# Gate columns beside W1 with routing one iteration later, POOL's products with D in the pair's own iteration, and expert rows filled up at the front

## What is computed

```python
mod = (silu(c) @ wmod).reshape(1, 6, 1, 512);  sa, ca, ga, sb, cb, gb = mod[:, 0], ..., mod[:, 5]
# the magnitudes of ga and gb are held at 0.25 or more
h = layernorm(x) * (1 + ca) + sa
x = x + ga * (tanh(h @ B.T) @ C.T + D * h)
h = layernorm(x) * (1 + cb) + sb
scores = sigmoid(h @ gate_w.T)                       # 2048 x 8
_, idx = top_k(scores + router_bias, 2)
w = take_along_axis(scores, idx); w = w / sum(w)
y_e = (silu(h @ W1[e]) * (h @ W3[e])) @ W2[e]        # inner width 352, for the 2 experts of a token
shared = (silu(h @ sw1.T) * (h @ sw3.T)) @ sw2.T     # inner width 704
x = x + gb * (sum_e w_e * y_e + shared)
```

## Time and profile before

| | us |
|---|---|
| median of 3 runs | 610.11 |
| the runs | 609.97, 610.11, 612.59 |
| the profiled execution | 610.75 |
| its span, first to last instruction | 609.1 |
| mean granted clock of TensorE | 0.981 of full |
| PE busy | 565.2 (93%), 3304 instructions |
| DVE busy | 321.6 (53%) |
| POOL busy | 242.4 (40%) |
| ACT busy | 178.1 (29%) |

### The profile page before, as it was taken

One profiled execution on the slowest core, in us unless ns is written; L12 is line 12 of the kernel. 1 busy time (PEld: TensorE's weight loads), 2 busy tenths in 40 slices (PEclk: granted clock), 3 DMA queues, 4 the chain that ended last, 5 costly groups with the idle time before them and its releaser, 6 DMA issues.

```text
span 609.1 us, 11649 instructions
## 1 busy us (share of the span) xinstructions
PE 565.2 (93%) x3304; PEld 508.9 (84%) x3305; DVE 321.6 (53%) x642; ACT 178.1 (29%) x332; POOL 242.4 (40%) x201
## 2 busy tenths in 40 slices
PE   4986899999999885999989999989999999999995
PEld 2655888988988774899979999979999998999994
DVE  3599788878876874432222222222222226666766
ACT  1344243344344131232222322223222322121220
POOL 1698674674683361340073500266160003322231
PEclk9998899999999988899999999999999999999999
DMA  8985193222222226952268632567662234554443
GB/s 312 369 278 207 52 346 123 87 103 97 75 104 104 102 91 223 345 209 96 85 216 317 230 121 80 161 216 268 239 224 71 69 101 143 163 170 151 141 140 116
DMA packets 37576, 102.72 MB, mean 169 GB/s; under 512 B 4272, under 2 KB 4272, under 8 KB 36656
## 3 DMA queue, kind: packets, MB, share of 16 engines
q1 hardware_dynamic: 27968, 53.65, 25.4%
q0 software_dynamic: 9152, 47.98, 22.1%
q10 hardware_dynamic: 432, 0.79, 0.3%
HBM read 71.73 MB, written 30.67 MB: 168 GB/s over the span
## 4 chain that ended last, share of the span: by engine, by line
PE 67%; issue 12%; DVE 9%; POOL 5%; DMA 4%; ACT 2%; SPq 1%; DVEq 0%; POOLq 0%; ACTq 0%
PE bank L808 11%; PE bank L810 11%; PE bank L809 11%; PE bank L822 6%; PE bank L824 6%; PE bank L823 6%; PE bank L794 4%; PE bank L829 3%; PE bank L899 2%; POOL wlo L474 2%; PE bank L764 2%; PE bank L763 2%; PE bank L765 2%; DMA whi<-w_all 2%; DVE sel L1087 1%
## 5 line engine op out<-in xcount | busy, mean ns | idle before, releaser
L808 PE MATMUL bank<-whi,thi 128*128 x416 | 140.2, 337 | 4.6 <-POOL wlo L474 4.6
L810 PE MATMUL bank<-whi,tlo 128*128 x416 | 135.2, 325 | 0.0
L809 PE MATMUL bank<-wlo,thi 128*128 x416 | 135.1, 325 | 0.0
L822 PE MATMUL bank<-whi,gth 128*128 (+1 forms) x204 | 81.6, 400 | 3.2 <-DVE gtl L1064 1.6
L808 PEld LDWEIGHTS bank<-whi,thi 128*128 128x128 f32 x416 | 79.1, 190 | 5.8 <-issue 5.8
L474 POOL TENSOR_TENSOR wlo<-raw,whi 128x1408 f32 (+3 forms) x21 | 69.0, 3308 | 35.4 <-DMA whi<-w_all 35.3
L1434 DVE TENSOR_TENSOR gbuf<-s,bank 128x352 f32<-128x352 f32 x52 | 27.0, 519 | 103.7 <-ACT s L742 103.4
L1438 DVE TENSOR_TENSOR gtl<-bank,gth 128x384 fp32r<-128x384 f32 x52 | 29.0, 558 | 97.8 <-ACT gth L746 97.8
L824 PE MATMUL bank<-whi,gtl 128*128 (+1 forms) x204 | 80.5, 395 | 0.0
L823 PE MATMUL bank<-wlo,gth 128*128 (+1 forms) x204 | 80.5, 395 | 0.0
L809 PEld LDWEIGHTS bank<-wlo,thi 128*128 128x128 f32 x416 | 79.3, 191 | 0.0
(11 more groups left out here) (180 smaller groups left out, 1046.0 us busy)
## 6 DMA issues: line engine op xcount, KB each, us to landing
raw<-w_all POOLq DMA_DIRECT2D x7, 2176.0 KB, 9.2
whi<-w_all POOLq DMA_DIRECT2D x14, 704.0 KB, 10.0
h<-xs_rows SPq DMA_DIRECT2D x36, 256.0 KB, 2.8
ys_rows<-tmpa SPq DMA_DIRECT2D x36, 256.0 KB, 2.1
x_all<-wmod SPq DMA_DIRECT2D x6, 1024.0 KB, 8.4
whi<-w_all POOLq DMA_DIRECT2D x7, 768.0 KB, 13.1
hs_rows<-h SPq DMA_DIRECT2D x8, 512.0 KB, 2.8
h<-hs_rows SPq DMA_DIRECT2D x16, 256.0 KB, 2.7
```

Of the source, the lines that this page charges most:

```text
L808: pe.matmul(dst, xh[:, j, a], wh, start=(m == 0), stop=False)
L809: pe.matmul(dst, xh[:, j, a], wl, start=False, stop=False)
L810: mm = pe.matmul(dst, xl[:, j, a], wh, start=False, stop=(m == KD - 1))
L822: pe.matmul(dst, gth[:, a], wh, start=(m == 0), stop=False)
```

## The change

Three parts.

**The gate.** The 8 gate columns are laid beside the 352 columns of W1 in slot A (`UPA = UP + E`), so that `up` of half 0 has 360 columns and the first 8 of its result are the gate's logits. ACT copies them out (`lg`) behind each silu, and makes the sigmoid at the end of the iteration. The 16 gate matmuls and the two `xtf` copies are left in one iteration only, that of the last pair (`it` = 10). Routing of pair p runs one iteration later: all of `route` and the scatter work on `it-4`, steps 7 to 11 stand together at the end of DVE's iteration, and PE's `ranks` stand behind the last `turn_g`. In iteration 10 the pairs 6 and 7 are both routed and both scattered.

**The term with D** of pair `it` is made in iteration `it`, behind `rs1`; before, it was made at the head of iteration `it+1`.

**The pads.** Each expert's rows now begin 128 rows further, and the zeros stand in the first 128 rows: one DMA of 2 MB near the start writes them for all experts. The first tile of an expert begins in the zeros (`lead`), which costs a few more small operations in `table_rows` and one in `routed`. The eight pads at the end of phase A are gone.

The core of the diff:

```diff
-PAD_ACT = 3
+UPA = UP + E
+SH = KD * E
...
+            sp.dma_start(xs[0:E * R, :].rearrange("(e r) d -> r e d", r=R)[0:P],
+                         zrow[:, :].unsqueeze(1).to_broadcast([P, E, D])).then_inc(s_pad, 16)
             sp.wait_ge(s_mod, 6)
...
-                if live(3, lo, hi):
-                    p = it - 3
+                if routes(lo, hi):
+                    p = it - 4
                     left = value(sp, p * 64)
                     sp.wait_ge(s_nat, p * 16 + 16)
...
+                if is_last(lo):
+                    sp.wait_ge(s_nat, NP * 16)
+                    sp.wait_ge(s_xd, NP)
+                    sp.dma_start(hrow[1], hs[(NP - 1) * 2 * P:NP * 2 * P, :].rearrange("(b p) d -> p b d", p=P)
...
-            pad(sp, 0, E - PAD_ACT, s_pad)
-            sp.wait_ge(s_pad, 16 * (E - PAD_ACT + 2))
-            sp.wait_ge(s_pad_act, 16 * PAD_ACT)
+            sp.wait_ge(s_pad, 48)
             sp.wait_ge(s_scat, 64 * NP)
...
             def body(it, lo, hi):
-                if lo > 2:
-                    with_d(it, lo, hi)
...
+                if lo > 2 and live(0, lo, hi):
+                    times_d(it)
+                    with_d(it)
...
+                if is_last(lo):
+                    scatter(it - 4, 0)
+                    scatter(it - 3, 1)
+                if routes(lo, hi) and not is_last(lo):
+                    scatter(it - 4, 0)
...
-                act.activation(s1[:, :], bank[2][:, 0:F], ACT.Silu).then_inc(q["A", "silu"], 1)
+                act.activation(s1[:, :], bank[2][:, E:E + F], ACT.Silu).then_inc(q["A", "silu"], 1)
+                if not is_last(lo):
+                    act.activation(lg[:, bass.ds(p * 2 + j, 1), :].rearrange("p a e -> p (a e)"), bank[2][:, 0:E],
+                                   ACT.Copy).then_inc(s_lg, 1)
...
                 if live(3, lo, hi):
                     hidden(it - 3, 1, lo)
+                    if not is_last(lo):
+                        p = it - 3
+                        act.wait_ge(s_lg, p * 2 + 2)
+                        act.activation(sc[:, bass.ds(p * 2, 2), :], lg[:, bass.ds(p * 2, 2), :],
+                                       ACT.Sigmoid).then_inc(s_sc, 1)
...
+                        if sec == "A":
+                            w, n = m * UPA + h * (E + F), F + (1 - h) * E
...
                 if live(3, lo, hi):
                     product_a(it - 3, 1, lo)
-                between(7, 8, 9)
                 if live(3, lo, hi):
                     finish_a(it - 3, 0, lo)
-                between(10)
                 if live(3, lo, hi):
                     low_a(it - 3, 1, lo)
-                between(11)
+                between(*range(KM + 1, KR))
```

More of the change, by code:

```diff
@@ L285, in live, with routes @@
             return lo - lag >= 0 and hi - lag < NP
-        def pad(eng, first, end, done):
-            eng.wait_ge(s_cnt, 1)
-            for e in range(first, end):
-                n = eng.value_load(ti[0:1, TB_N + e:TB_N + e + 1], min_val=0, max_val=T)
-                eng.dma_start(xs[bass.ds(n + e * R, P), :], zrow[:, :]).then_inc(done, 16)
+        def routes(lo, hi):
+            return lo - 4 >= 0 and hi - 4 < NP - 1
         def steps(eng, iters, step):
@@ L931, in body @@
                 if live(3, lo, hi):
+                    if not is_last(lo):
+                        pe.wait_ge(s_lg, (it - 3) * 2 + 1)
                     up("A", it - 3, 1, 0)
[L933 to L934 removed]
                 if live(3, lo, hi):
@@ L943, in body @@
                     turn_g(bank[5]).then_inc(q["A", "gt"], 1)
+                if routes(lo, hi) and not is_last(lo):
+                    ranks(it - 4, bank[7])
             pe.wait_ge(s_silb, KD)
```

204 lines of the change are left out of this document (108 added, 96 removed).

## The result

The changed kernel takes **612.63 us** (median of 20 runs, 610.63 to 614.24), the kernel before 610.50 (median of 20, 609.27 to 613.11). The ratio is **1.0029**, interval 1.0019 to 1.0038: slower by 0.3 %, within the 0.5 % that the prediction calls no change. Forecast were 607.0 and a range of 602.8 to 610.9; the time lies above it, and on the other side of the kernel before. The profiled execution of the changed kernel took 610.72 (span 609.0), 1.9 under its median. A second profile of the same kernel (experiment e13, span 612.2, 613.88 us) lies 1.3 over it, so I read both.

What follows compares the result with a forecast made beforehand. PE was taken to bound most inner iterations of phase A. Terms 0 + 1.5 + 3.4 - 2.2 + 0.35 = 3.05, say 3.1 us gained, brought the median from 610.11 to 607.0, range 602.8 to 610.9.

Steps and rivals of the forecast that it cites:

- Iterations 5 to 8: Phase A: `ra` held by POOL until 2.1, `up` starting at 4.6; gain 0.86 us each, 3.4 in all.
- `ra`, `pos` and `idx` take 0.5: DVE, iterations 5 to 8: these routing steps take 0.5 us after POOL's hold ends at 2.1, so `tlo` starts at 2.6.
- 5.3, where almost nothing is left: Iterations 5 to 8: late end of the forecast start of `up`, 5.3 us, with almost no gain left; 4.6 was taken.
- The first rival: Iterations 5 to 8: the hold misses the path, giving 1.5 us each, 2.6 more in all, 604.4; chance 0.18.
- Iteration 4: Phase A: `up` starts at 3.95 instead of 5.41, with wider half and hidden `ranks` counted; gain 1.5 us.
- The rival of a dearer switch of tables: ACT, iterations 4 to 8: table switch costs a wait behind `gth` too; 0.25 us gain each, 610.7; chance 0.03.
- Iteration 3: PE waits for the weights' third low half; a POOL product coming between offsets DVE's missing routing steps; gain 0.
- the third rival: DVE is held in more places, at iteration 3 by two products and at its head: 608.3 to 611.5; chance 0.12.
- Iteration 9: Phase A: POOL's work 0.8 us later, PE's wait 3.5, then slow clock taken as 1.5; loss 2.2 us.
- the rule of the port: Iteration 9: by it `sel` passes between two POOL instructions, gaining about 1.6 us; not used, the measured row was followed.
- The end: Iteration 10 to phase S: pads go, eight scatters land at 24.7 instead of pads at 25.07; gain 0.35 us.
- 4.4 would be there: End of phase A: far end of the gain, 4.4 us, if the scatters of pair 6 cost nothing.

Runs made afterwards that it cites:

- e13: Changed kernel again, nothing changed, on another chip: 613.57 us, ratio 1.0038.
- e8: Changed kernel with the routing's `ra`, `pos` and `idx` moved behind `xal` of the next iteration: 605.62 us, ratio 0.9917.
- e1: Kernel before with only the zeros written near the start and the eight pads gone; gate, routing and POOL's products as before: 606.72 us, ratio 0.9925.
- e7: Changed kernel with the second weight slot's low halves ahead of POOL's scatter, behind `slo` in iteration 8 and the first `gtl` in iteration 9: 603.25 us.
- e6: Changed kernel with separate buffers and lists of rows for the scatters of the last three pairs: 608.79 us, ratio 0.997.
- e10: Changed kernel with DVE's low half of the last weight piece in iteration 3 made ahead of `tbuf` and `slo`: 605.69 us, ratio 0.9912.
- e12: Changed kernel with an already fulfilled wait on POOL ahead of the last train of scatters: 607.75 us, ratio 0.9948.
- e17: Changed kernel again, nothing changed, beside another run on one chip: 612.44 us, ratio 1.0034.
- e9: Changed kernel with 32 more small PE transposes, read by nothing, ahead of iteration 3: 610.13 us, ratio 0.9994.
- e3: Changed kernel with the second weight slot's low halves ahead of POOL's scatter, right behind `rs2` in iteration 8: 613.04 us, ratio 1.0034.

## Why the prediction was wrong, point by point

**Iterations 5 to 8: right mechanism, mis-sized term.** The forecast was that `ra` is held until POOL's end, 2.1 into the iteration, and that `up` starts at 4.6. POOL ended at 2.28 and `ra` was held until 2.34. But `tlo` started at 3.37 and not at 2.6: `pos` and `idx` took until 2.96 with the steps between them, and another 0.41 went before `tlo`. The term "`ra`, `pos` and `idx` take 0.5" was too small: from the end of the hold to `tlo` it was 1.03. `tlo` and the first `xal` end at 5.3. The forecast had named this end ("5.3, where almost nothing is left") and did not take it. Iteration 5 gave its 0.87: the hold there was only 0.11 shorter, but from its end to `tlo` went 0.55, and not 1.03. Iterations 6 to 8 gave 1.1 in place of 2.6. The first rival, that the hold misses the path, had 0.18; e8 shows what it would have been worth: 20.8 us per iteration.

**Iteration 4** gave 1.62 to 1.64 for 1.5, with the table load where it was forecast. The rival of a dearer switch of tables fell: the load starts at 140.98, 0.02 behind the end of `gth`, and the sigmoid at 142.28, 0.02 behind the end of the load. The drain of some 1.4 us that the Trainium skill has (ScalarE: Activation LUTs, What ACT_TABLE_LOAD costs) is not seen there.

**Iteration 3** was put at nothing. In both profiles `down` starts 1.25 us earlier (72.64 and 72.65 for 73.89 in the earlier trace rows), because DVE's low half does: the product of POOL that was to come between did not (`wlo` at 70.83 follows `slo` at once). It is not earlier still because DVE's second step on `h` (`h<-h,rs`) waits for POOL's `rs2`, which stands behind POOL's products of pair 2. The two operations of the first step (`h<-x_all`) were held by the last of these, 3.63 us (4.50 in the second profile) for 1.42, but were done 0.59 and 0.87 us before `rs2`: a hold of the third rival ("DVE is held in more places", 0.12), and one that cost nothing. PE came to its wait 2.7 and 3.8 us earlier than before, and so waited 1.83 and 2.97 us for 0.36; in the second profile the clock fell behind it and turned the gain of 1.25 into a loss of 0.33. e1, whose iteration 3 is that of the kernel before, has such a wait too, 2.00 us.

**Iteration 9** lost 1.41 in the first profile, and 2.56 in the second, for 2.2: idle time of 3.55 for 3.5, and the clock as forecast, 0.93 and 0.86. e7 shows the cause. What the prediction worked out from the rule of the port (the Trainium skill, SBUF — State Buffer, Who interferes with whom), that `sel` would pass between two POOL instructions, does not come out here: `sel` was again held across both, 5.96 us, and the row decided rightly.

**The end** is the step that failed. Its sum was good: 28.67 - 0.35 = 28.32 forecast from iteration 10 to phase S, 28.1 to 28.4 measured in the six profiles of e6 to e10 and e12, where the update was on time. But in the changed kernel's own three profiles PE's update came 4.3 to 5.2 us late, and 31.8 to 32.1 were measured: a loss of 3.2 to 3.4 for a gain of 0.35. Nothing in the profile before showed it and no rival held it; it is 3.5 to 3.8 of the 5.6 us between 607.0 and 612.63, and why the update is late stays open. Behind it stands a second oversight, of weight rather than of sum: e1 shows that the zeros were worth 4.2 us at the end, and that the second train and the gate of the last pair took all but 0.35 of that back. I had both numbers (the last scatter landed by 233 in the earlier trace rows, "4.4 would be there") and did not ask what the change would be without its other half.

**The clock** makes up most of the difference between the two profiles. The sum stood on one execution; e13 has 3.4 us more at 1.2 GHz in iteration 3 and 3.4 more in iteration 9, the changed kernel's third profile (e17) 3.4 more in iteration 9, and both more from iteration 10 on. Idle time of PE goes with it each time: 2.97 us in iteration 3, 3.55 in iteration 9, 3.3 behind the late update.

The range ended at 610.9. For the end alone it had 1.5 us lost as its far side, where 3.2 to 3.4 were lost.

## What to carry to other kernels

Work that is taken off the bounding engine is a gain only down to the next engine's chain, so ask of that chain's every step what holds it. Here most waits behind DVE and POOL had been hidden by the gate's 1.7 us, and the gain came only when existing work was moved: `ra` behind `xal`, the low halves beside DVE operations that read PSUM, iteration 3's piece ahead of `tbuf`. With the trains' own buffers that ended 15 us under the kernel before. Take a change with several parts apart before judging it: of this one, one part alone gave 0.75 %, and the rest, until it was placed rightly, took back all of that where the update was late (1.0 %), and 0.2 to 0.7 % where it was on time (e12, e9).

## What the runs showed of the hardware that I had not expected

- PE's semaphore update came 4.3 to 5.4 us behind the end of its matmul by the profile in eight profiles, while POOL had indirect DMAs under way; in e7, e10 and e12, with the same eight scatters, it didn't. A matmul's end in the trace is then no proof that its reader was released; the reader's wait reads "remote".
- A DVE operation of 16 elements with two inputs in SBUF waited 5.96 us across two POOL operations of some 3.2 us, and `ahead` 7.00 in e8; `h` of 512 elements took 3.71 in e3, in place of 0.74. `gbuf`, with one input in PSUM, took its usual 0.52 us beside the same two operations in e7.
- The same idle time of 3.55 us in iteration 9 went with 3.4 us at 1.2 GHz in some executions and with 6.8 in others; iteration 9 took 22.8 to 23.1 us with the one and 23.9 to 24.3 with the other.
